# A schedule by tables: the first and last batch row scanned by column halves, and every step placed on its own

## The chip, the cores and the metric

One core of one Trainium2 chip runs the kernel. The metric is device time of one execution in microseconds: the median of three runs is 2578.41 us (2577.72 to 2578.85). Lower is better.

## The reference

The input is x of 16 batch rows by 1024 positions by 256 channels. A "row" below is one of the 16 batch rows, "columns" are its 1024 positions.

```python
x = x + 0.5 * ffn(layernorm(x))        # FFN 1
x = x + ssm(layernorm(x))              # a state-space layer
x = x + 0.5 * ffn(layernorm(x))        # FFN 2

def ffn(x):                            # hidden width 768, weights are integers / 127
    return (silu(x @ wg.T) * (x @ wu.T)) @ wd.T

def ssm(x):                            # E=256 channels, N=16 states, R=64
    z, params = x @ W_z.T, x @ W_params.T
    dt = softplus(params[..., :R] @ W_dt.T + b_dt)
    u = silu(causal_conv4(x))          # 4 taps, by channel
    A = -exp(A_log)                    # (E, N)
    a = exp(dt[..., None] * A); bt = (a - 1) / (A + 1e-10)
    # h[t] = a[t-1]*h[t-1] + bt[t-1]*u[t-1], h[0] = bt[0]*u[0], for each channel and state
    y = sum_n(C[..., n] * h[..., n])
    return ((y + u * D) * silu(z)) @ W_out.T
```

## The kernel before, in words

Channels lie on the 128 partitions in EH = 2 groups (h), columns on the free axis, in NC = 2 chunks (c) of CH = 512. For each row b and each of the 16 states s and 2 groups h there is one **unit** of the scan, 512 units in all:

- ScalarE `ex` writes exp(dt * A) of 1024 columns into one of 6 slots of `ring` (L781).
- VectorE `scan` runs TENSOR_TENSOR_SCAN over 1024 columns into PSUM (`g_bank`, L977), from `du_bank`, which ScalarE's `db` (L768) fills once for each group from GpSimd's `d`.
- VectorE `cm` multiplies by 1/A and by the C row that a DMA (`bc`) has spread over all partitions (L1008).
- GpSimd `cm` adds the product to `acc` (L856).

Around the scan of row b lie all other steps. A step is named by kind, then FFN or norm number where there is one, then row, chunk and so on. `ld` loads x (SP). `ln` (VectorE, L929 and L933), `lr` (GpSimd, L804 and L806: 1/sqrt), `ls` (VectorE, L938), `lx` (ScalarE, L624: the normed rows), `T` (TensorE transposes, L508/L511) and `Te` (ScalarE copies out) are one layer norm; `Ts` and `Tl` make a second fp16 part for the FFNs. `ga` and `up` (TensorE, L531) are the FFN's two inputs by blocks m = 0 to 5, `si` its silu, `sh` (VectorE, L948) or `sc` and `hp` (ScalarE and GpSimd, m = 0, 2, 4) the product; `dn` (TensorE, L543, 24 matmuls each) its output, `rs` and `rp` the residual. `pm`, `pe`, `cv` (L582), `us`, `dt`, `da`, `dl`, `dp`, `rm` (L597), `ai` (VectorE, L965 and L968), `u0`, `dt0`, `z`, `zs` are the state-space layer ahead of the scan; `gate` (GpSimd), `op` (TensorE, L553), `rc`, `ra` come behind it. `cw` and `bc` are the DMAs of C, `st` stores. The matmul jobs share 4 PSUM banks, each held until the step that reads it is done.

There is one order of all steps, `K.order`, made by `schedule()`: every step gets a time in units of the scan (row b begins at 32 b), the list is sorted, and each engine takes its own steps from the list in that order. Engines wait only by semaphores. So a step that waits holds back all that stands behind it on its engine, however ready that is.

Before, the times come from few numbers: a start for each kind and chunk (`AT`), a fixed pace over m (`PACE`), and lags (`LAG`). All silu steps are moved to the next slot of a grid of 4 units, `ex`, `da` and `dl` to another such grid, so that ScalarE changes its table of functions twice in 4 units (L611). All rows have the same times. SP loads x of row b into `x_in` once row b-1 is through with it, and `x_fin` holds the row that leaves.

Of the kernel before, what the change touches and what calls it, by code (L numbers as in the profile page):

```python
# [38 lines left out]
P = 128  # L39
# [37 lines left out]
AT = {  # L77
# [6 lines left out]
}  # L84

PACE = {
    "gu1": 0.732, "gu2": 1.087,
}

LAG = {  # L90
# [11 lines left out]
def phase(t, start):  # L102
    return CYCLE * ((t - start) // CYCLE) + start


def schedule():
    out = []

    def at(t, *ev):
        out.append((t, len(out), ev))  # L110

    def put(t0, name, i, *ev):
        at(t0 + AT[name][i], *ev)

    def after(t0, name, lag, i, *ev):
        at(t0 + AT[name][i] + LAG[lag][i], *ev)

    def rows(t0, f, b):
        for c in range(NC):
            put(t0, f"ln{f}", c, "ln", f, b, c)  # L120
            for kind in ("lr", "ls", "lx", "T", "Te") + (("Ts", "Tl") if f != 2 else ()):
                after(t0, f"ln{f}", f"{kind}{f}", c, kind, f, b, c)

    def curved(t, pe, act):
        p = phase(t, AT["silu"][0])
        at(p + 0.01 * (t - p), *pe)
        at(p + 0.01 * (t - p) + 0.005, *act)

    def ffn(t0, f, b):
        for c in range(NC):  # L130
            for m in range(HM):
                t = t0 + AT[f"gu{f}"][c] + m * PACE[f"gu{f}"]
                curved(t, ("ga", f, b, c, m), ("si", f, b, c, m))
                at(t + LAG["up"][0], "up", f, b, c, m)
                if m in POOLED:
                    at(t + LAG["up"][0] + LAG["sc"][0], "sc", f, b, c, m)
                    at(t + LAG["up"][0] + LAG["hp"][0], "hp", f, b, c, m)
                else:
                    at(t + LAG["up"][0] + LAG["sh"][0], "sh", f, b, c, m)
            for jp in range(2):  # L140
                put(t0, f"dn{f}", 2 * c + jp, "dn", f, b, c, jp)
                after(t0, f"dn{f}", f"rs{f}", 2 * c + jp, "rs", f, b, c, jp)
                if f == 1:
                    after(t0, f"dn{f}", "rp1", 2 * c + jp, "rp", b, c, jp)
# [893 lines left out]
```

## Time and profile before

| | |
|---|---|
| median of the runs | 2578.41 us |
| the profiled execution: its time | 2578.04 us |
| its span | 2576.0 us |
| first scan of row 0 | 135.5 us after the span's start |
| first scan of row 1 / of row 15 | 272.4 / 2374.0 us |
| `db` of row 2's second group / row 13's second group (starts) | 493.6 / 2145.8 us |
| end of the last product of the scan | 2503.3 us |

The profiled execution lies 2.0 us above its span, which is what is around the span, and 0.4 us below the median. The profile counts times from the span's start. The two cuts in the row before the last are starts of `db` 11 rows apart, so that the stretch between them is 11 whole rows.

### The profile page before, as it was taken

Reading aid. Unit: us, or ns where it says so; the run is one execution under the profiler, and the core shown is the slowest. Engines: PE = TensorE matmul, PEld = TensorE weight load, DVE = VectorE, ACT = ScalarE, POOL = GpSimd, SP = SyncE. Lnnn points to the kernel's source line nnn. Section 1 sums busy time; section 2 is a strip of 40 time slices with the busy share of each in tenths; the row PEclk is TensorE's granted clock in tenths of the full one; section 3 lists DMA queues with packets and bytes.
Section 4 is the critical chain, followed back from the end, with each engine's and each line's share of the span. In section 5 each row is a group of like instructions: output and inputs, shape, how many; then the busy total and the mean of one; then the engine's idle time right before and its main releaser. Section 6 shows DMA issues by size and latency. Waiting matters only on the chain.

```text
span 2576.0 us, 28487 instructions
## 1 busy us (share of the span) xinstructions
PE 2290.1 (89%) x9220; PEld 1382.1 (54%) x9220; DVE 2287.3 (89%) x2294; ACT 1984.9 (77%) x2830; POOL 2074.4 (81%) x1286
## 2 busy tenths in 40 slices
PE   6877799899998989999898999999899999988478
PEld 3443455556465555646555564655556565555245
DVE  2189999999999999999999999999999999999981
ACT  4668787887878788787877878787787878776643
POOL 2367988888798888879888888988888898888772
PEclk9887999999999999999999999999999999998689
DMA  2133334334343433434343343434334343433430
GB/s 73 34 118 120 131 116 130 128 118 139 108 147 116 131 130 117 139 108 147 121 132 121 119 139 107 148 121 133 122 119 139 107 147 122 133 114 115 140 115 17
DMA packets 112025, 307.97 MB, mean 120 GB/s; under 512 B 11201, under 2 KB 45314, under 8 KB 111874
## 3 DMA queue, kind: packets, MB, share of 16 engines
q1 hardware_dynamic: 111874, 306.13, 36.3%
q8 instruction: 73, 1.20, 0.2%
q14 instruction: 78, 0.64, 0.1%
HBM read 288.27 MB, written 17.83 MB: 119 GB/s over the span
## 4 chain that ended last, share of the span: by engine, by line
PE 50%; ACT 19%; DVE 13%; issue 10%; POOL 7%; DMA 1%; DVEq 0%; SPq 0%; POOLq 0%; ACTq 0%
PE work L543 19%; PE work L531 12%; DVE g_bank L977 7%; PE work L582 6%; ACT ring L781 5%; POOL acc L856 4%; PE work L511 4%; DVE ring L1008 4%; ACT normed L624 4%; PE work L553 2%; ACT L611 2%; PE work L560 2%; PE work L590 2%; ACT xt_lo L662 1%; PE work L597 1%
## 5 line engine op out<-in xcount | busy, mean ns | idle before, releaser
L856 POOL TENSOR_TENSOR acc<-acc,ring 128x1024 f32<-128x1024 f32 x512 | 1211.0, 2365 | 175.3 <-DVE ring L1008 154.8
L977 DVE TENSOR_TENSOR_SCAN g_bank<-du_bank,ring 128x1024 f32<-128x1024 f32 x512 | 1174.6, 2294 | 29.9 <-ACT du_bank L768 15.8
L543 PE MATMUL work<-wd_t,hid 128*128 128x256 f32 x3072 | 691.7, 386 | 22.2 <-DVE hid L948 18.5
L1008 DVE SCALAR_TENSOR_TENSOR ring<-g_bank,inv_a,ring 128x1024 f32<-128x1024 f32 x512 | 654.9, 1279 | 11.3
L543 PEld LDWEIGHTS work<-wd_t,hid 128*128 128x128 f32 x3072 | 596.3, 194 | 117.9 <-DVE hid L948 21.3
L781 ACT ACTIVATE ring<-dt,a_coef 128x1024 f32<-128x1024 f32 x512 | 548.0, 1138 | 1.5 <-DVE g_bank L977 0.2
L825 POOL TENSOR_TENSOR hid<-hid,sil 128x512 f32<-128x512 f32 x192 | 244.6, 1274 | 136.3 <-ACT hid L683 136.3
L531 PE MATMUL work<-xt_hi,wg_t 128*128 128x512 f16 x768 | 311.1, 405 | 42.7 <-ACT xt L649 15.7
L611 ACT ACT_TABLE_LOAD x257 | 329.7, 1283 | 4.6
L531 PE MATMUL work<-xt_lo,wg_t 128*128 128x512 f16 x768 | 310.8, 405 | 0.0
L531 PE MATMUL work<-xt_hi,wu_t 128*128 128x512 f16 x768 | 302.4, 394 | 5.3 <-ACT sil L675 5.2
L531 PE MATMUL work<-xt_lo,wu_t 128*128 128x512 f16 x768 | 302.3, 394 | 0.0
L675 ACT ACTIVATE sil<-work 128x512 f32<-128x512 f32 x384 | 220.5, 598 | 102.1 <-PE work L531 98.0
L582 PE MATMUL work<-xt,tap_diag 128*128 128x512 f32 x512 | 232.2, 596 | 0.0
L511 PE MATMUL work<-ident,normed 128*128 128x128 f32 x1024 | 139.1, 292 | 89.0 <-ACT normed L624 89.0
L948 DVE SCALAR_TENSOR_TENSOR hid<-sil,work 128x512 f32<-128x512 f32 x192 | 130.3, 678 | 93.6 <-PE work L531 93.6
L511 PEld LDWEIGHTS work<-ident,normed 128*128 128x128 f32 x1024 | 128.4, 203 | 121.8 <-ACT normed L624 108.5
L531 PEld LDWEIGHTS work<-xt_hi,wg_t 128*128 128x128 f16 x768 | 78.3, 102 | 179.5 <-issue 32.8
L582 PEld LDWEIGHTS work<-xt,tap_diag 128*128 128x128 f32 x512 | 95.5, 191 | 109.3 <-issue 97.7
L531 PEld LDWEIGHTS work<-xt_hi,wu_t 128*128 128x128 f16 x768 | 76.8, 100 | 130.3 <-issue 40.6
L691 ACT ACTIVATE x_mid<-work 128x512 f32<-128x512 f32 x64 | 37.7, 588 | 139.5 <-PE work L543 139.5
L683 ACT ACTIVATE hid<-work 128x512 f32<-128x512 f32 x192 | 112.3, 585 | 37.0 <-PE work L531 37.0
(90 smaller groups left out, 2829.2 us busy)
## 6 DMA issues: line engine op xcount, KB each, us to landing
ring<-c_rows SPq DMA_DIRECT2D x512, 512.0 KB, 3.7
x_in<-L_attn_x SPq DMA_DIRECT2D x32, 512.0 KB, 4.6
out<-x_fin SPq DMA_DIRECT2D x32, 512.0 KB, 4.0
c_rows<-params SPq DMA_DIRECT2D x32, 32.0 KB, 3.4
ring<-L_ffn_w_gate SPq DMA_DIRECT2D x1, 768.0 KB, 5.8
ring<-L_ffn_w_up SPq DMA_DIRECT2D x1, 768.0 KB, 7.2
ring<-L_ffn_w_down SPq DMA_DIRECT2D x1, 768.0 KB, 10.5
wz_t<-L_attn_W_z SPq DMA_DIRECT2D x1, 256.0 KB
```

The source lines that it names most:

```text
L511: last = pe.matmul(dst[:, j * P:(j + 1) * P], block, ident[:], start=(j == 0), stop=(j == TJ - 1))
L531: last = pe.matmul(dst[:], w[:, k, m * P:(m + 1) * P], part_[:, k, :], start=(k == 0 and i == 0), stop=(k == EH - 1 and i == 1))
L543: last = pe.matmul(dst[:, j * E:(j + 1) * E], hid[:, K.unit[f, bt, c, m] % HIDS, t:t + P], wd_t[:, m, :], start=(m == 0), stop=(m == HM - 1))
L582: last = pe.matmul(dst[:], tap_diag[:, h, k, :], xt[:, h, k + c * CH:k + (c + 1) * CH], start=(k == 0), stop=(k == KW - 1))
L611: nc.scalar.preload_act_table_set(name)
L675: nc.scalar.activation(sil[:, K.at["silu", ev][1] % SILUS, :], bank(job)[:], ACT.Silu, scale=GATE_SCALE).then_inc(freed(job), 1)
L781: nc.scalar.activation(decay[:, slot, :], dt[bt % 2][:, h, 0:L], ACT.Exp, scale=a_coef[:, h, s:s + 1]).then_inc(S["decay"], 1)
L825: nc.gpsimd.tensor_tensor(v, v, sil[:, k, :], ALU.mult).then_inc(S["product"], 1)
L856: nc.gpsimd.tensor_tensor(acc[bt % 2][:, h, :], acc[bt % 2][:, h, :], cg[:, slot, :], ALU.add).then_inc(S["summed"], 1)
L948: nc.vector.scalar_tensor_tensor(hid[:, i, :], sil[:, K.at["silu", silu][1] % SILUS, :], H_SCALE, bank(job)[:], ALU.mult, ALU.mult).then_i ...
L977: scan = nc.vector.tensor_tensor_scan(g_bank[:], du_bank[:], decay[:, a, :], 0.0, ALU.add, ALU.mult)
L1008: nc.vector.scalar_tensor_tensor(cg[:, k, :], g_bank[:], inv_a[:, h, s:s + 1], spread[:, k_c, :], ALU.mult, ALU.mult).then_inc(S["weighted ...
```

## The change

**The tables.** `AT`, `PACE`, `LAG` and both grids go. `ROW` has a position for every step of a row; `HEAD` replaces those of row 0 up to the scan, `TAIL` those of row 15 behind it. `schedule()` only adds 32 b and sorts. The number of steps is the same (5920).

**Paired rows.** In rows 0 and 15 (`paired`) a unit is no longer one group by 1024 columns: it is both groups by 512 columns. Units 0 to 15 (p = 0) do the first half of the columns, units 16 to 31 (p = 1) the second. A unit has two scans, two exps and two products of 512 columns, and one addition on GpSimd of 2 x 512. The state at column 511 is kept in `carry` by one VectorE copy in each unit of p = 0, and is the start of the scan of p = 1. With it, `d`, `db`, `gate` go by halves of the columns, and the waits of `u0`, `dt0`, `ex`, `ai`, `op` ask for one half only.

**Buffers.** Row 1's x goes into `x_fin`, so that it can be loaded at once; row 15's result goes into `x_in`.

```diff
-AT = { "scan0": [0.67, -0.01], "cm": [0.75], "bc": [-4.95], ...
-PACE = { "gu1": 0.732, "gu2": 1.087, }
-LAG = { ...
+ROW = {
+    "ln2": [-23.104, -15.157],
+    "lr2": [-23.088, -15.505],
+    "ls2": [-21.644, -14.717],
+    "lx2": [-20.845, -14.043],
+    "T2": [-18.333, -12.53],
...
+HEAD = {
+    "ln2": [-25.298, -5.26],
...
+TAIL = {
+    "op": [19.781, 20.832, 43.795, 44.13],
...
+def paired(b):
+    return b in (0, B - 1)
...
+        for name, ev in row_events(b):
+            table = HEAD if b == 0 and name in HEAD else TAIL if b == B - 1 and name in TAIL else ROW
+            i = seen[name] = seen.get(name, -1) + 1
+            out.append((round(SLOTS * b + table[name][i], 3), len(out), ev))
...
-                    if s == 0 and h == 0:
+                    if s == 0 and p == 0:
                         wait(act, "dt_first", ("dt0", bt))
+                    elif s == 0 and paired(bt):
+                        for h in range(EH):
+                            wait(act, "sp_sum", ("dp", bt, h, p))
...
+                    d = decay[:, K.number[ev[1:]] % DECAYS, :]
+                    for h in range(EH) if paired(bt) else (p,):
+                        dst, t = (halves(d)[:, h, :], slice(p * CH, (p + 1) * CH)) if paired(bt) else (d, slice(0, L))
+                        nc.scalar.activation(dst, dt[bt % 2][:, h, t], ACT.Exp,
+                                             scale=a_coef[:, h, s:s + 1]).then_inc(S["decay"], 1)
...
+                        for h in range(EH) if pair else (p,):
+                            less = EH - 1 - h if pair else 0
+                            wait(dve, "weighted", was, less=less if was and paired(was[1]) else 0)
+                            wait(dve, "decay", ("ex",) + ev[1:], less=less)
+                            g, du_h, d_h, v_h = (halves(x)[:, h, :] if pair else x for x in (g_bank[:], du_bank[:], d, v))
+                            first = [carry[:, k, s, h, :] if pair and p else 0.0 for k in range(2)]
+                            scan = nc.vector.tensor_tensor_scan(g, du_h, d_h, first[0], ALU.add, ALU.mult)
...
+                            if pair and p == 0 and h == 0:
+                                wait(dve, "scanned", ("scan",) + ev[1:])
+                                if not with_tiny:
+                                    nc.vector.tensor_copy(carry[:, 0, s, :, :],
+                                                          halves(g_bank[:])[:, :, CH - 1:CH]).then_inc(S["carried"], 1)
...
-                    wait(pe, "gated", ("gate", bt, EH - 1))
+                    wait(pe, "gated", ("gate", bt, piece(bt, EH - 1, jp // 2)))
...
+        def x_of(b):
+            return x_fin if b == 1 else x_in
+        def fin(b):
+            return x_in if b == B - 1 else x_fin
```

Sorted, the old and new positions give these orders, which the prediction refers to.

```
round the norm of FFN 1's output (row b+1 beside the scan of row b), first chunk
VectorE  old: scan9 ls3 ln2 cm9 scan10 sh ls2 cm10       new: ln2 cm9 sh scan10 cm10 ls2
GpSimd   old: cm8 hp cm9 lr2 cm10                        new: cm8 ra lr2 cm9 hp cm10
TensorE  old: up4 up5 T2 ga(FFN 2)0 ga1 dn dn pm         new: up5 ga(FFN 2)0 ga1 T2 dn dn pm
the `ai` of row b+1
VectorE  old: scan11 sh ai ai ln1 ai ai cm11             new: sh cm10 ai scan11 ai ai cm11 ai
TensorE  old: rm dt dt rm rm rm up                       new: dt rm dt rm rm up up ga rm

head, row 0, chunk 0 unless said, new
TensorE: T1, all 12 ga/up with 4 of chunk 1 among them, dn dn, up ga up up, T2, ga, pm,
         cv(h1), up, dt(h0), ga, cv(h0), up, dt(h1), rm, z, T1 of row 1, dn(c1), up ga ga of row 1, dn(c1)
ScalarE: us(h1), da dl (h0), si si (c1), us(h0), lx1 of row 1, u0, sc, Te, zs, Tl, da(h1), rs(c1), sc,
         dl(h1), si si, lx1, rs(c1), dt0, si, ex0 ex1, Te, db
         (old: both chunks and groups of da, dl and us, then dt0, ex0 to ex3, db)
tail, row 15, new
TensorE: op(c0), T3(c0) and 6 ga/up of it, row 14's last dn dn, the other 6 ga/up, op(c1), dn(c0), T3(c1), 12 ga/up, dn(c1)
         (old: row 14's last dn dn, op x4, T3(c0), FFN 2 of both chunks)
```

Between silu steps and exp or log steps, the old order has 257 changes of ScalarE's table, 16 in each middle row; the new one has 289, 18 in each.

## Rows read from the trace of the kernel before

**Rows 1.** The page: busy time of each engine, and VectorE in 40 slices

```profile
PE 2290.1 (89%) x9220; PEld 1382.1 (54%) x9220; DVE 2287.3 (89%) x2294; ACT 1984.9 (77%) x2830; POOL 2074.4 (81%) x1286
...
DVE  2189999999999999999999999999999999999981
```

**Rows 2.** Stretches: start:end, length, busy (x) per engine, PEclk, DMA share, GB/s

```profile
493.60:2145.80 1652.20, 1541.26 (x6338) 934.41 (x6337) 1569.37 (x1564) 1356.29 (x1936) 1425.83 (x881) 0.96 0.39 127
135.50:272.30 136.80, 101.56 (x316) 54.64 (x316) 132.20 (x114) 100.86 (x137) 110.00 (x64) 0.79 0.38 127
2373.40:2503.30 129.90, 73.46 (x261) 46.12 (x260) 123.16 (x94) 69.76 (x84) 97.32 (x50) 0.72 0.40 130
2503.30:2576.00 72.70, 60.95 (x284) 42.77 (x282) 11.99 (x30) 21.27 (x38) 19.77 (x16) 0.95 0.07 22
```

**Rows 3.** VectorE's waits in the 11 middle rows: total us, times, longest

```profile
DVE hid L948 <- PE work L531: 23.0, 29, 1.2
DVE shift L938 <- POOL rstd L806: 19.9, 15, 1.7
DVE acc L965 <- PE work L597: 13.9, 22, 0.9
DVE g_bank L977 <- ACT du_bank L768: 6.4, 14, 0.8
```

**Rows 4.** VectorE's groups there: busy us, mean ns, idle before

```profile
L977 DVE TENSOR_TENSOR_SCAN g_bank<-du_bank,ring 128x1024 f32<-128x1024 f32 x353 | 809.7, 2294 | 14.5 <-ACT du_bank L768 6.4
L1008 DVE SCALAR_TENSOR_TENSOR ring<-g_bank,inv_a,ring 128x1024 f32<-128x1024 f32 x352 | 450.1, 1279 | 7.5
L948 DVE SCALAR_TENSOR_TENSOR hid<-sil,work 128x512 f32<-128x512 f32 x132 | 89.5, 678 | 23.0 <-PE work L531 23.0
...
L938 DVE SCALAR_TENSOR_TENSOR shift<-meanvar,rstd 128x4 f32<-128x4 f32 x67 | 32.9, 492 | 20.0 <-POOL rstd L806 19.9
```

**Rows 5.** Timeline round one `ls` of FFN 1's output, all engines

```profile
1369.70 2.35 POOL L856 TENSOR_TENSOR acc<-acc,ring 128x1024 f32<-128x1024 f32 x1
...
1372.01 0.20 POOL L804 TENSOR_TENSOR rstd<-meanvar,eps 128x4 f32<-128x4 f32 x1
...
1373.35 0.16 DVE L938 SCALAR_TENSOR_TENSOR shift<-meanvar,rstd 128x4 f32<-128x4 f32 x1 [1.72 <-POOL rstd L806]
...
1376.21 0.98 PE L508 MATMUL work<-ident,normed 128*128 128x128 f32 x7 [3.39 <-ACT normed L624]
```

**Rows 6.** ScalarE's timeline in the head

```profile
64.88 1.06 ACT L649 ACTIVATE xt<-work 128x512 f32<-128x512 f32 x2
...
94.66 1.28 ACT L611 ACT_TABLE_LOAD   x1
95.96 0.60 ACT L744 ACTIVATE dt<-work 128x512 f32<-128x512 f32 x1
...
102.65 2.06 ACT L624 ACTIVATE normed<-x_in,shift,rstd 128x256 f32<-128x256 f32 x4
```

**Rows 7.** The chain that ended last, in the head: start, us, what

```profile
31.58 8.63 PE work L531 x40
40.21 10.36 PE work L543 x48
...
53.41 0.43 POOL x_mid L832
...
77.78 3.45 PE work L582 x8
...
135.52 2.31 DVE g_bank L977
```

**Rows 8.** The same chain in the tail

```profile
2494.85 13.45 PE work L543 x48
2508.30 5.36 PE work L553 x24
```

**Rows 9.** GpSimd's costliest group, whole run

```profile
L856 POOL TENSOR_TENSOR acc<-acc,ring 128x1024 f32<-128x1024 f32 x512 | 1211.0, 2365 | 175.3 <-DVE ring L1008 154.8 <-ACT params L735 6.5
```

More of the change, by code:

```diff
@@ L106, in schedule @@
 def schedule():
     out = []
[L109 to L144, printed above, removed]
@@ L201, in __init__ @@
         place = {ev: i for i, ev in enumerate(self.order)}
+        self.units = [(b, s, p) for b in range(B) for p in range(EH) for s in range(N)]
+        self.number = {unit: i for i, unit in enumerate(self.units)}
         uses, until = [0] * BANKS, [-1] * BANKS
@@ L398, in earlier, with halves, part, shaped @@
         def earlier(ev, back):
-            q = ev[1] * SLOTS + ev[3] * N + ev[2] - back
-            return ("cm", q // SLOTS, q % N, q % SLOTS // N)
+            i = K.number[ev[1:]] - back
+            return ("cm",) + K.units[i] if i >= 0 else None
+        def halves(t):
+            return t.rearrange("p (h t) -> p h t", h=EH)
+        def part(b, p, t, first=0):
+            if paired(b):
+                return t[:, :, first + p * CH:first + (p + 1) * CH]
+            return t[:, p, first:first + L]
+        def shaped(b, t):
+            return halves(t) if paired(b) else t
+        def x_of(b):
+            return x_fin if b == 1 else x_in
+        def fin(b):
+            return x_in if b == B - 1 else x_fin
         def bank(job):
@@ L452, in _ @@
                     wait(sp, "free", ("pm", bt, c))
-                    for i in range(SPREADS):
-                        q = EH * N - 1 - i
-                        wait(sp, f"c_spread{(bt * SLOTS + q - 2 * SLOTS) % SPREADS}", ("bc", bt - 2, q % N, q // N))
+                    for unit in [u for u in K.units if u[0] == bt - 2][-SPREADS:]:
+                        wait(sp, f"c_spread{K.number[unit] % SPREADS}", ("bc",) + unit)
                     sp.dma_start(c_rows[bt % 2, :, c * CH:(c + 1) * CH],
@@ L719, in _ @@
                     _, bt = ev
-                    wait(act, "free", ("cv", bt, EH - 1, 0))
+                    for h in range(EH):
+                        wait(act, "free", ("cv", bt, h, 0))
                     nc.scalar.activation(u[bt % 2][:, :, 1:2], u[bt % 2][:, :, 2:3], ACT.Copy).then_inc(S["u_first"], 1)
@@ L841, in _ @@
                 elif kind == "gate":
-                    _, bt, h = ev
-                    wait(pool, "summed", ("cm", bt, N - 1, h))
-                    for c in range(NC):
-                        wait(pool, "free", ("z", bt, h, c))
-                    nc.gpsimd.tensor_tensor(acc[bt % 2][:, h, :], acc[bt % 2][:, h, :], zs[:, h, :],
-                                            ALU.mult).then_inc(S["gated"], 1)
+                    _, bt, p = ev
+                    wait(pool, "summed", ("cm", bt, N - 1, p))
@@ L849, in _ @@
+                    for k in range(NC):
+                        wait(pool, "free", ("z", bt, k, p) if paired(bt) else ("z", bt, p, k))
+                    v = part(bt, p, acc[bt % 2])
+                    nc.gpsimd.tensor_tensor(v, v, part(bt, p, zs), ALU.mult).then_inc(S["gated"], 1)
                 elif kind == "cm":
-                    _, bt, s, h = ev
+                    _, bt, s, p = ev
                     wait(pool, "weighted", ev)
                     if s == 0:
-                        wait(pool, "acc_begun", ("ai", bt, h, NC - 1))
+                        for k in range(EH):
+                            wait(pool, "acc_begun", ("ai", bt, k, p) if paired(bt) else ("ai", bt, p, k))
@@ L970, in program @@
                     elif kind == "scan":
-                        _, bt, s, h = ev
-                        a = K.at["decay", ("ex",) + ev[1:]][1] % DECAYS
-                        wait(dve, "weighted", earlier(ev, 1))
-                        wait(dve, "decay", ("ex",) + ev[1:])
+                        _, bt, s, p = ev
+                        i, pair = K.number[ev[1:]], paired(bt)
+                        d, v = decay[:, i % DECAYS, :], cg[:, i % TERMS, :]
+                        was = earlier(ev, 1)
```

334 lines of the change are left out of this document (209 added, 125 removed), and 87 rows, old and new, of tables (AT, LAG, ROW, TAIL).

## The prediction

> **What bounds the kernel now.** I begin with the page: busy times and slices [rows 1]. VectorE is at 9 or more tenths in every slice from the third on; only the first slices and the last are poor. So the run has three parts: a head up to the first scan (135.5 us), sixteen rows of scan, and a tail behind the last product (2503.3 to 2576 us). The stretches give their sizes [rows 2]: 11 middle rows take 1652.2 us, 150.2 each; row 0 takes 136.8, row 15 129.9, the tail 72.7. In the middle rows VectorE works 142.7 us of 150.2 and TensorE 140.1. One is the bound and the other is right behind it, with ScalarE at 123.3 and GpSimd at 129.6. VectorE stands idle 7.5 us a row.
>
> Where these 7.5 us are is in the waits [rows 3]: 23.0 us for TensorE's `up`, 19.9 for GpSimd's 1/sqrt, 13.9 for `rm`, 6.4 for `du_bank`: 63.2 over 11 rows, 5.7 a row. The other 1.8 are small gaps between instructions, which an order doesn't touch. So 5.7 us a row is the most that a better order can win from waits, and 144.5 the shortest row. Inside the busy time there is a little more: `ls` takes 492 ns on average and the second `ai` 1274 [rows 4], but one `ls` that started late took 160 ns [rows 5]. These are stalls inside instructions, some 2 us a row for `ls` (6 x 0.33), and I expect nothing of them for the sum.
>
> **Part 1, the head.** I follow chunk 0 in the new orders. The first chunk's residual is ready at 53.84 [rows 7]. New, four instead of two jobs of chunk 1 stand ahead of `dn`: two more of four matmuls at 0.216 us (8.63 us for 40) [rows 7], 1.7 us, so 55.6. Norm, transposes and the copy to `xt` took from 53.84 to 65.94 [rows 6, 7], 12.1 us, and I keep that: 67.7. `pm` (half of a `cv`, 1.7), one `ga` (0.9) and the first `cv` (3.45 [rows 7]) end at 73.8. Before, the second chunk's `dn` of 10.36 us [rows 7] came in between; that is what the halves save first. From here ScalarE's queue counts. A plain step is 0.6 us, a table load 1.28, `lx` 2.06, one chunk of `da` and `dl` 3.35 (6.69 for two) [rows 6]. Up to `Te` of row 1: us 0.6, load 1.3, da and dl 3.35, load 1.3, two si 1.2, us 0.6, lx 2.1, u0 and sc 0.8: 85.0. It waits for TensorE's T1, behind three ga/up, two dt, cv, rm, z and T1 itself: 73.8 + 13.6 = 87.4. Then Te 1.2, zs 0.6, Tl 1.2, load 1.3, da 1.5: 93.2. `rs` needs `dn` of chunk 1: TensorE is there at 93.5. rs, sc, dl: 96.9. Load, two si, lx: 101.4; the second rs waits until 101.4 + 0.6. dt0 and si 0.8, load 1.3, four exps of half width 2.3, Te 1.2, db 1.0: the first scan is at about 109 instead of 135.5. **-26.5 us**, and with the four banks in play I give it 105 to 120. Nothing of chunk 1 vanishes: two `ai`, its norm and `ls` now lie among row 0's scans, 2 x 1.8 + 1.8 + 0.2 = **+5.5** on VectorE. TensorE's later work (some 60 us for the rest of row 0's second half up to its last `rm`) has the 65 us of the first 16 units: little slack, an upper side for the range.
>
> **Part 2, the price of a pair.** A unit was 2.294 + 1.279 us [rows 4] and becomes two scans and two products of 512 columns. A product-like instruction of 512 columns takes 678 ns [rows 4], so two cost 77 ns more than one of 1024. The trace has no scan of 512 columns: from below the same 77 ns, from above the whole 160 ns that an instruction of 4 columns takes [rows 5]. I take 120, plus 50 for two more starts: 0.25 us a unit, 8 us a row. The 16 copies into `carry` are tiny: 0.16 each, 2.6. **+10.6 us** in row 0 and in row 15 each; bounds 5 and 16. Less than none is excluded, as nothing is removed.
>
> The Trainium skill (VectorE: DVE Perf Modes, "The TRN2 errata") puts an instruction's fixed part at about 150 cycles, 0.16 us; by it the pair would cost 12.5 us a row and the sum would be 4 us longer. The product's rows show half of that.
>
> ScalarE's exps also double in number, and it has 26.9 us free in a row; `bc` moves the same bytes in one row of halves; GpSimd's additions keep their 2.37 us [rows 9].
>
> **Part 3, the fourteen rows between.** Here the order alone changes. I look at the largest single wait. VectorE's `ls` stood 1.72 us for GpSimd, whose 1/sqrt began at 1372.01, behind an addition to `acc` that started at 1369.70 [rows 5]; between `ln2` and `ls2` VectorE's own order has a product, a scan and an `sh`. And TensorE then stood 3.39 us before `T2` for the same chain. New, `lr2` stands ahead of that addition, `ls2` behind a whole product more, and `T2` behind an `up` and two `ga`. That wait goes, 1.8 us a row with its smaller kin, and TensorE wins 3 us with it, which comes back to VectorE as earlier `up`s. Of the wait for `up` (2.1 a row) I take 1.1 as gone. `rm`: new, the four `ai` are spread, but the last `rm` stands behind two `up` and a `ga`; 1.3 a row, of which I take 0.3. `du_bank`: 0.6, I take 0.3. Together 3.5 of 5.7 us a row. The cover for all this is TensorE, which would be busy 140.1 of 146.7. Two more table loads a row, 2.6 us, lie on ScalarE and are hidden by its 26.9 free microseconds. **-49 us** for 14 rows; ends: 0 and -80.
>
> The `x_fin` and `x_in` edits cost nothing, since the loads are off the path; without that cover they would cost one load's landing.
>
> **Part 4, the tail.** Before, 72.7 us: row 14's last `dn` on TensorE until 2508.3, four `op` 5.36, a norm, two chunks of FFN 2 [rows 2, 8]. New, row 15's first half is through `gate`, `op` and norm by then. Behind the last product TensorE has: `dn` of row 14, 5.0; 6 ga/up 5.2; two `op` 2.7; `dn` of chunk 0 10.4 [rows 7]; T3 and its second part about 4; 12 ga/up 10.4; `dn` 10.4; then `rs` and the store 4.7. That is 53. The second half's own chain (addition, gate, op, norm) takes about 20 us and is done when TensorE reaches T3. **-19.7 us**; bounds 47 and 62 for the tail. The first half's norm moves into row 15's scans, +2.0.
>
> **The sum.** Row 1 begins at 109 + 136.8 + 10.6 + 5.5 = 261.9 instead of 272.3: -10.4. Rows 1 to 14: -49. Row 15: +12.6. Tail: -19.7. Together -66.5 from the span of 2576.0: 2509.5, and 2.0 around it: 2511.5. The profiled run lies 0.4 us under the median of the runs, so I say **2512 us**.
>
> **The rivals.**
> A: the middle rows win nothing. For it: TensorE is only 2.6 us a row behind VectorE, and at its clock between two levels (PEclk 0.96) it may be the true bound; each wait that goes comes back as one of VectorE for TensorE. Against: TensorE stands idle 10.1 us a row, much of it in the chain of `ls`. Then 2512 + 49 = 2561.
> B: all 63 us of waits per 11 rows go: 14 x 5.7 = 80, and 2481.
> C: the head gains nothing, since a ScalarE step with chunk 1's work ahead of it (both `rs` stand ahead of `dt0`) holds the first scan at 135: 2512 + 26 = 2538.
> D, slower: ScalarE's two more table loads fall where TensorE waits for a bank, so that 2.6 us a row come onto VectorE's path and no wait goes. It decides from 1.8 us a row upward: without part 3 the change is -17.5, so 14 rows must lose 22 to come out 0.2% slower. With 2.6: 2561 + 36 = 2597. Against it: between load and next step there is 0.02 us [rows 6], and ScalarE's free time is ten times the addition.
> The Trainium skill (ScalarE: Activation LUTs, "What ACT_TABLE_LOAD costs") adds 1.38 us of drain to each load; by it D's price would be 5.3 us a row. This trace disagrees: the step behind the load starts at once.
>
> **Chances.** Forecast 0.45, A 0.18, B 0.2, C 0.1, D 0.07. The range takes B with a good head at its low side and A with a dear pair at the high: 2460 to 2570; D lies outside. About 0.2% (5 us) is what a measurement can tell from no change. Faster 0.91, same 0.03, slower 0.06.
>
> **What would show it.** In the new profile: the first scan at 105 to 120 us; half scans of 1.2 us and copies of 0.1 to 0.2; starts of row 1 and row 15's `db` 14 x 146.7 us apart; `ls` without a wait of 1.7 us; 289 table loads; a tail of 53 us. I am wrong if the row stays at 150 (A), if VectorE's waits for `up` grow as those for 1/sqrt go, or if row 0 is longer than 153 us because TensorE is late with its second half.

## The result, and the profile after

The changed kernel takes 2454.95 us (median of 4 runs, 2452.45 to 2457.36) against 2578.06 beside it (2575.96 to 2578.85). The ratio is 0.9524, interval 0.9507 to 0.9540. I had said 2512 with a range from 2460 to 2570: the sign is right, but the gain is 123 us and not 66, and the time lies 5 us below the range.

The page after, whose rows answer to [rows 1], and with them the clock:

```profile
PE 2258.3 (92%) x9220; PEld 1359.8 (55%) x9220; DVE 2282.8 (93%) x2454; ACT 2030.5 (83%) x2926; POOL 2073.5 (84%) x1286
...
DVE  2599999999999999999999999999999999999993
...
PEclk9997999999999899999999899999999999999789
```

VectorE's busy time is the same as before (2287.3), so the 120 us of span that went were all time in which it stood. Four stretches show where. First row 0 up to the first scan of row 1, then fourteen rows, row 15, and the tail; the columns are those of [rows 2]:

```profile
102.14:248.31 146.17, 114.30 (x358) 57.00 (x356) 141.37 (x198) 123.73 (x195) 117.42 (x71) 0.85 0.23 68
248.31:2277.76 2029.45, 1941.13 (x7999) 1172.60 (x7998) 1978.43 (x1968) 1746.99 (x2476) 1809.05 (x1115) 0.97 0.39 130
2277.76:2406.20 128.44, 82.99 (x332) 53.90 (x332) 128.00 (x181) 85.23 (x130) 102.55 (x56) 0.83 0.23 70
2406.20:2455.60 49.40, 43.31 (x206) 30.35 (x204) 9.26 (x20) 12.66 (x23) 13.54 (x10) 0.98 0.10 33
```

The same stretch of fourteen rows before:

```profile
272.39:2373.96 2101.57, 1954.92 (x7993) 1182.51 (x7994) 1993.35 (x1968) 1716.43 (x2445) 1811.41 (x1116) 0.96 0.39 126
```

| part | before, us | after | change | forecast |
|---|---|---|---|---|
| up to the first scan | 135.5 | 102.1 | -33.4 | -26.5 |
| row 0 | 136.9 | 146.2 | +9.3 | +16.1 |
| rows 1 to 14 | 2101.6 | 2029.5 | -72.1 | -49 |
| row 15 | 129.3 | 128.4 | -0.9 | +12.6 |
| tail | 72.7 | 49.4 | -23.3 | -19.7 |
| span | 2576.0 | 2455.6 | -120.4 | -66.5 |

The miss is in rows 0 and 15 (20 us) and in the middle rows (23 us); 10 us are head and tail. VectorE's waits in 11 middle rows after, against [rows 3]:

```profile
DVE hid L1099 <- PE work L662: 11.6, 16, 1.5
DVE acc L1118 <- PE work L728: 6.7, 6, 2.6
DVE x_fin L1107 <- PE work L674: 3.4, 4, 1.4
```

That is 21.7 us where 63.2 stood. The list of TensorE leads to another step; its waits in those 11 rows, before:

```profile
PE work L508 <- ACT normed L624: 50.2, 22, 3.4
PE work L511 <- ACT normed L624: 21.3, 22, 1.0
PE work L531 <- ACT xt L649: 11.8, 11, 1.7
PE work L573 <- ACT xt L649: 8.6, 11, 0.8
PE work L597 <- ACT sp_r L747: 7.6, 22, 0.4
```

and after:

```profile
PE work L674 <- DVE hid L1099: 21.5, 9, 3.3
PE work L662 <- ACT xt_lo L793: 8.0, 11, 0.7
PE work L662 <- ACT sil L806: 7.6, 11, 0.7
PE work L662 <- ACT hid L814: 7.6, 11, 0.7
PE work L639 <- ACT normed L755: 6.9, 11, 0.6
```

Before, TensorE stood 71.5 us ahead of its transposes for ScalarE's `lx` (`normed`); after, 6.9. The sum of its waits is 110.6 before (two more, 5.9 and 5.2) and 65.4 after (four more: 5.0, 4.6, 4.0, 0.2). The row stretch is 52.3 us shorter (1652.2 against 1599.9, from `db` to `db`), the waits are 45 us less, and TensorE's busy time is 8.8 less, at a granted clock of 0.97 of full speed instead of 0.96. These two make up the 52.3 us to within 2. That says where the time was, and not yet why it went: an engine's waits and work always add up to its stretch. VectorE's account closes as well (41.5 us of waits and 9.4 of work less). Which list leads to the cause, the runs below have to show.

One pair (a unit of two column halves) after, on VectorE's timeline:

```profile
102.14 2.35 DVE L1142 TENSOR_TENSOR_SCAN g_bank<-du_bank,ring 128x512 f32<-128x512 f32 x2 [0.53 <-ACT du_bank L903]
104.40 0.73 DVE L1178 SCALAR_TENSOR_TENSOR ring<-g_bank,inv_a,ring 128x512 f32<-128x512 f32 x1
105.04 0.15 DVE L1183 COPY carry<-g_bank 128x2 f32<-128x2 f32 x1
105.11 0.74 DVE L1178 SCALAR_TENSOR_TENSOR ring<-g_bank,inv_a,ring 128x512 f32<-128x512 f32 x1
105.76 1.22 DVE L1142 TENSOR_TENSOR_SCAN g_bank<-du_bank,ring 128x512 f32<-128x512 f32 x1
```

A pair with its copy goes from 102.14 to 105.76: 3.62 us. A bare unit of 1024 columns takes 3.65 from start to start. Each of the five instructions begins before the one ahead of it is recorded as ended.

### The profile page after: what moved, and what is told of

Same layout as the page of the kernel before. It is cut to its first block and busy times, and to the rows that moved or that the text cites. A ratio compares the mean times of both kernels' runs of the same rounds, so it can differ in the third digit from the quotient of the medians.

```text
span 2455.6 us, 28769 instructions
## 1 busy us (share of the span) xinstructions
PE 2258.3 (92%) x9220; PEld 1359.8 (55%) x9220; DVE 2282.8 (93%) x2454; ACT 2030.5 (83%) x2926; POOL 2073.5 (84%) x1286
## 5 line engine op out<-in xcount | busy, mean ns | idle before, releaser
L1142 DVE TENSOR_TENSOR_SCAN g_bank<-du_bank,ring 128x1024 f32<-128x1024 f32 (+1 forms) x512 | 1100.6, 2155 | 7.3 <-ACT du_bank L903 0.5
L1178 DVE SCALAR_TENSOR_TENSOR ring<-g_bank,inv_a,ring 128x1024 f32<-128x1024 f32 (+1 forms) x576 | 664.6, 1159 | 11.4
L674 PEld LDWEIGHTS work<-wd_t,hid 128*128 128x128 f32 x3072 | 590.0, 193 | 153.4 <-DVE hid L1099 43.6
L921 ACT ACTIVATE ring<-dt,a_coef 128x1024 f32<-128x1024 f32 (+1 forms) x576 | 577.4, 1047 | 7.0 <-DVE g_bank L1142 4.1
L662 PE MATMUL work<-xt_hi,wg_t 128*128 128x512 f16 x768 | 299.7, 390 | 29.4 <-ACT sil L806 14.5
L662 PE MATMUL work<-xt_lo,wg_t 128*128 128x512 f16 x768 | 298.8, 389 | 0.0
L964 POOL TENSOR_TENSOR hid<-hid,sil 128x512 f32<-128x512 f32 x192 | 249.7, 1301 | 53.6 <-ACT hid L814 38.9
L684 PE MATMUL work<-wo_t,acc 128*128 128x256 f32 x512 | 119.0, 386 | 11.3 <-POOL acc L987 6.1
```

Source lines behind the costliest of these rows:

```text
L662: last = pe.matmul(dst[:], w[:, k, m * P:(m + 1) * P], part_[:, k, :], start=(k == 0 and i == 0), stop=(k == EH - 1 and i == 1))
L674: last = pe.matmul(dst[:, j * E:(j + 1) * E], hid[:, K.unit[f, bt, c, m] % HIDS, t:t + P], wd_t[:, m, :], start=(m == 0), stop=(m == HM - 1))
L921: nc.scalar.activation(dst, dt[bt % 2][:, h, t], ACT.Exp, scale=a_coef[:, h, s:s + 1]).then_inc(S["decay"], 1)
L964: nc.gpsimd.tensor_tensor(v, v, sil[:, k, :], ALU.mult).then_inc(S["product"], 1)
L1142: scan = nc.vector.tensor_tensor_scan(g, du_h, d_h, first[0], ALU.add, ALU.mult)
L1178: nc.vector.scalar_tensor_tensor(v, g, inv_a[:, h, s:s + 1], c_row, ALU.mult, ALU.mult).then_inc(S["weighted"], 1)
```

## The experiments

**The pair alone.** The old order and its three tables, with the new loops for rows 0 and 15:

```diff
-ROW, HEAD, TAIL and their schedule()
+AT, PACE, LAG and their schedule()
 def paired(b): return b in (0, B - 1)
```

> Rows 0 and 15 by column halves and the new buffers, but every step at its old position. The old positions put the whole of row 0 ahead of its first scan and row 15's op behind its last gate, so nothing can start earlier; what is left is the price of 64 paired units. Theory F (a pair is free, because the fixed part of an instruction hides behind an independent one before it; in the new trace a paired unit comes every 3.62 to 3.66 us, one of 1024 columns every 3.65): 2578 us, give or take 3. The prediction's price (0.25 us a unit and 0.16 a copy, 10.6 a row): 2599 us. Theory F says that half of the miss in rows 0 and 15 is this term.

2582.14 us (2580.74 to 2582.97, 10 runs), ratio 1.0017, interval 1.0008 to 1.0027. Row 0 of it, from its first scan to that of row 1, and row 15, from its first scan to the last product:

```profile
138.14:275.97 137.83, 99.64 (x317) 55.03 (x318) 134.55 (x194) 106.47 (x166) 109.89 (x65) 0.80 0.22 71
2377.77:2508.14 130.37, 71.72 (x267) 46.11 (x266) 125.98 (x173) 74.79 (x111) 96.75 (x50) 0.76 0.22 69
```

Row 0 is 1.0 us longer than the 136.9 of before and row 15 1.1 longer than 129.3, where I had put 10.6 each. Of the 4.6 us in the span 2.6 are the first scan, which begins at 138.1. Pairs alone gain nothing, and cost about 1 us a row.

**The order alone.** `ROW` for all sixteen rows, no pairs:

```diff
-    return b in (0, B - 1)
+    return False
-            table = HEAD if b == 0 and name in HEAD else TAIL if ... else ROW
+            table = ROW
```

> Only the table ROW, for all 16 rows, no pairs. If the middle rows' 5.15 us a row come from the order inside a row and from nothing at the ends, 14 rows give -72, and rows 0 and 15 some more: 2495 to 2510 us. Rival (the middle gains because the early head lets TensorE run ahead): the rows stay near 150 and the time near 2560.

2494.39 us (2493.89 to 2498.31), ratio 0.9684, interval 0.9668 to 0.9700. Rows 1 to 14 take 144.7 us each from `db` to `db`, against 145.0 in the changed kernel, so the middle's gain is all here. The tail is 73.8 us, near the 72.7 of before.

**Without the head's table, and without the tail's.**

```diff
-HEAD if b == 0 and name in HEAD else TAIL if ... else ROW
+TAIL if b == B - 1 and name in TAIL else ROW      # the first
+HEAD if b == 0 and name in HEAD else ROW          # the second
```

> The changed kernel, but row 0 has the positions of ROW up to its scan, too; pairs and TAIL stay. If HEAD is what brings the first scan from 135.5 to 102.1 us, this loses most of 33 us less what row 0 then saves in work moved: 2478 to 2490 us, first scan at about 130. Rival (pairs alone, by their narrower waits, start the scan early): 2455 to 2462.

> The changed kernel, but row 15 has the positions of ROW behind its scan too; pairs and HEAD stay. If TAIL is what shortens the tail from 72.7 to 49.4 us: 2476 to 2480 us, a tail of some 72 us. Rival (the narrower waits of op alone shorten it): under 2465.

Without `HEAD` 2473.50 us (2470.26 to 2479.44), ratio 0.9601, interval 0.9584 to 0.9618. The first `db` starts at 130.3 instead of 101.1, but its row 0 is 137.6 us long from `db` to `db`, against 145.3: `HEAD` brings the scan forward by 29 us and gives 18.5 in the end. 7.7 us go back into row 0, which takes over chunk 1's work. Another 5.0 are in rows 1 to 14, which are that much shorter without `HEAD` (2025.0 us against 2030.0), and no run says why. Without `TAIL` 2476.77 us (2474.43 to 2478.82), ratio 0.9608, interval 0.9592 to 0.9624; the tail is 69.0 us. So the two tables for the edges carry 40 us. In the old order the pairs gave nothing without them; the two tables without pairs were not run.

**One step moved before.** My text put 1.8 us a row on `ls2` waiting for `lr2`, so I moved `lr2` alone:

```diff
-    "lr2": [0.22, 0.11],
+    "lr2": [0.05, 0.11],
```

> The kernel before with one lag changed: GpSimd's lr2 of the first chunk stands ahead of the addition to acc, not behind it (0.22 becomes 0.05). This takes away the 1.72 us wait of ls in each row and nothing else. Theory V (VectorE is the bound, a wait of it is worth its length): 16 x 1.7 = 27 us, so 2551. Rival T (TensorE is right behind, the wait comes back as waits for up or rm): under 10 us, 2568 to 2578.

2577.41 us (2573.94 to 2578.95, 10 runs), ratio 0.9998, interval 0.9988 to 1.0007. VectorE's wait for 1/sqrt falls from 19.9 to 2.7 us in 11 rows, and nothing is won. Its timeline at the place of [rows 5]:

```profile
1369.75 2.35 POOL L856 TENSOR_TENSOR acc<-acc,ring 128x1024 f32<-128x1024 f32 x1
...
1370.33 1.78 DVE L938 SCALAR_TENSOR_TENSOR shift<-meanvar,rstd 128x4 f32<-128x4 f32 x1
...
1370.52 1.28 ACT L611 ACT_TABLE_LOAD   x1
...
1371.82 1.15 ACT L781 ACTIVATE ring<-dt,a_coef 128x1024 f32<-128x1024 f32 x1
...
1372.88 2.06 ACT L624 ACTIVATE normed<-x_mid,shift,rstd 128x256 f32<-128x256 f32 x4
...
1374.98 1.09 PE L508 MATMUL work<-ident,normed 128*128 128x128 f32 x8 [3.39 <-ACT normed L624]
```

Two things are to be seen. `ls` (here the 4-column product at L938) starts 0.58 us after a GpSimd addition and ends with it: the wait has become a stall inside the instruction (its mean rises from 492 to 749 ns). And it didn't matter: ScalarE has a table load and an `ex` ahead of `lx`, and works through them without a pause, so that `lx` comes 0.77 us after `ls` has ended. TensorE stands 3.39 us before `T2`, as in [rows 5]. TensorE's whole list of waits is as before (50.2 and 21.3 for `normed`).

**The same step moved back in the changed kernel.**

```diff
-    "lr2": [-23.088, -15.505],
+    "lr2": [-22.65, -15.505],
```

> The changed kernel with lr2 of the first chunk put back behind that addition. The new VectorE order has a product, an sh, a scan and a product between ln2 and ls2, 5.5 us, and product, addition and 1/sqrt take 1.3 + 2.4 + 1.3 = 5.0, so by the rows no wait should come back: 2455 to 2460. Rival (the place of lr2 is what won the 1.8 us a row): 2455 + 26 = 2481.

2458.94 us (2453.16 to 2461.18), ratio 0.9532, interval 0.9516 to 0.9548: it costs nothing that can be told.

**Pairs in all rows, and pairs in series.**

```diff
 def paired(b):
-    return b in (0, B - 1)
+    return True
```

and, on top of it, each half's product right behind its own scan:

```diff
-scan h=0, scan h=1, product h=0, product h=1
+scan h=0, product h=0, scan h=1, product h=1
```

> The changed kernel with every row scanned by column halves, 512 paired units instead of 64. Theory F (a pair is free on VectorE): 2450 to 2465, if ScalarE's 512 more exps (about 2 us a row) stay hidden. The prediction's price of 10.6 us a row: 14 x 10.6 = 148 more, 2603.

> As all_rows_paired, but VectorE's four instructions of a unit stand as scan, product, scan, product, each product right behind the scan that it reads; the same instructions and numbers. Theory F says the pair is free because neighbours that don't depend on each other overlap by some 0.09 us while a dependent one starts 0.03 late: two dependent neighbours more in a unit, 2 x 0.12 x 512 = 120 us slower than all_rows_paired. Rival (half instructions are simply cheap, in whatever order): the same time as all_rows_paired, within 10 us.

2530.82 us (2530.36 to 2531.22), ratio 0.9818, interval 0.9802 to 0.9835; in series 2697.26 us (2692.45 to 2699.37), ratio 1.0466, interval 1.0449 to 1.0484. With pairs everywhere a row is 149.8 us, and VectorE is busy in 98% of it:

```profile
468.30:2123.60 1655.30, 1545.38 (x6337) 919.84 (x6336) 1623.30 (x2443) 1441.50 (x2310) 1423.97 (x881) 0.97 0.23 71
```

So a pair costs 1 us a row at the edges, and 5 in the middle, between my two expectations. Counting the neighbours explains most of it. In the kernel before, 26 of row 0's 32 products come directly behind their scan, and 25 scans directly behind a product; each of them starts 0.035 us late, and in pairs it starts some 0.085 early. In the changed kernel's 11 middle rows it is 253 of 352 products and 132 scans, so 35 places a row instead of 51: other instructions stand between, and a pair has less to hide. And `ls` is back at 473 ns from 175, 1.8 us a row. In series a bare unit takes 4.04 us, and the kernel 166 us more than with interleaved halves, where I had expected 120:

```profile
1245.36 1.23 DVE L1142 TENSOR_TENSOR_SCAN g_bank<-du_bank,ring 128x512 f32<-128x512 f32 x1
1246.62 0.75 DVE L1178 SCALAR_TENSOR_TENSOR ring<-g_bank,inv_a,ring 128x512 f32<-128x512 f32 x1
1247.29 1.22 DVE L1185 TENSOR_TENSOR_SCAN g_bank<-du_bank,ring 128x512 f32<-128x512 f32 x1
1248.55 0.75 DVE L1178 SCALAR_TENSOR_TENSOR ring<-g_bank,inv_a,ring 128x512 f32<-128x512 f32 x1
1249.21 0.15 DVE L1191 COPY carry<-g_bank 128x2 f32<-128x2 f32 x1
1249.40 1.23 DVE L1142 TENSOR_TENSOR_SCAN g_bank<-du_bank,ring 128x512 f32<-128x512 f32 x1
```

A product that needs the scan just ahead of it starts 0.03 us after the scan's end (1246.59 to 1246.62). A scan that needs nothing of the product ahead starts 0.08 us before the product's end. The order of the four decides what halves cost: these two runs have the same instructions, two to a scan and two to a product.

**`ls` rewritten.** To take its stall away, four instructions with one input column and a scalar replace it:

```diff
-nc.vector.scalar_tensor_tensor(shift[:, slot, :], meanvar[:, slot, :, 0], -1.0, rstd[:, slot, :], ...)
+for j in range(TJ):
+    nc.vector.tensor_scalar(shift[:, slot, j:j + 1], meanvar[:, slot, j, 0:1], -1.0,
+                            rstd[:, slot, j:j + 1], ALU.mult, ALU.mult)
```

> The kernel before with ls written as four tensor_scalar instructions, the one factor as a scalar per partition, so that none reads two tensors. In the trace of before an ls that meets a GpSimd instruction ends when that ends (1431.71 + 1.03 = 1432.74, GpSimd's ended at 1432.72). Theory L (the two engines lock each other out, and the lock costs VectorE its time): ls falls from 492 ns to some 0.25 us for all four, 2 us a row less: 2578 - 25 = 2553. Rival (as with lr2, the time is spent elsewhere): 2578.

> Both edits of ls in the kernel before: lr2 ahead of the addition, and ls as four instructions. Moving lr2 alone turned 17 us of waits into 16 us of longer ls instructions. Theory L: with the lock gone too, wait and stall are both won, 19.9 + 22 us in 11 rows, some 55 in 16: 2525 to 2535. Rival T (TensorE is the bound right behind): no faster than before_ls_alone by more than 5 us.

2581.17 us (2579.34 to 2582.94, 10 runs), ratio 1.0013, interval 1.0004 to 1.0023; with `lr2` moved too 2578.59 us (2576.59 to 2578.88), ratio 1.0002, interval 0.9992 to 1.0011. The four take 37 us in 11 rows where the one took 32.9, so VectorE was not relieved, and these runs don't decide by themselves. In all four kernels with the old order the 11 rows stay at 1651.4 to 1652.2 us, while VectorE's work in them goes from 1569 to 1584.

**No lock in the changed kernel.** `ls` as above, and the first product behind `rm` left in its PSUM bank, so that the second reads only one operand from SBUF:

```diff
-first ai:  t <- bank * u        second ai: t <- u * D - t
+first ai:  bank <- bank * u     second ai: t <- u * D - bank
```

> The changed kernel with ls as four instructions and with the first product of ai left in its PSUM bank, so that the second reads one tensor of SBUF and one of PSUM; same results. There the second ai takes 1665 ns instead of the 750 of one that meets no GpSimd instruction: 64 x 0.9 = 58 us of VectorE's time. Theory L with VectorE as the bound: 2455 - 45 = 2410. Theory T (TensorE, busy 96% in the middle rows, takes over): 2435 to 2450.

2460.12 us (2459.07 to 2464.66), ratio 0.9541, interval 0.9525 to 0.9557. The second `ai` falls from 1727 to 748 ns, and the wait for `rm` rises to 30.9 us in 11 rows. VectorE works 19.6 us less in them (the four instructions of `ls` take part of the relief back), and they are 3.2 us shorter; the first scan is 6 us later. Nothing is won, which neither theory had.

**Fewer matmuls.** The last of six hidden blocks is left out of both down projections, so a sixth of the hidden width is missing from the output:

```diff
 for m in range(HM):
+    if m == HM - 1: continue
     last = pe.matmul(dst, hid[:, unit[m], t:t + P], wd_t[:, m, :], ...)
```

> The changed kernel without the last of the six blocks that each dn sums (the output lacks a sixth of the hidden width): 7 us a row less for TensorE, nothing less for the others. If VectorE is the bound of the middle rows, only its waits for TensorE go, 21.7 us in 11 rows, and half the ends' matmuls: 2420 to 2435. If TensorE is the bound: 16 x 7 = 112 less, under 2380.

2452.54 us (2450.23 to 2455.58), ratio 0.9510, interval 0.9494 to 0.9526: within what can be told from the changed kernel, and outside both of my ranges. Two groups of TensorE in 11 rows, here and in the changed kernel:

```profile
L676 PE MATMUL work<-wd_t,hid 128*128 128x256 f32 x1760 | 395.0, 382 | 18.1 <-DVE x_fin L1109 10.7 <-DVE hid L1101 7.4
...
L715 PE MATMUL work<-xt,tap_diag 128*128 128x512 f32 x353 | 162.3, 607 | 27.1 <-ACT sil L808 27.1
```

```profile
L674 PE MATMUL work<-wd_t,hid 128*128 128x256 f32 x2112 | 475.3, 384 | 21.5 <-DVE hid L1099 21.5
...
L713 PE MATMUL work<-xt,tap_diag 128*128 128x512 f32 x354 | 158.8, 595 | 4.6 <-ACT sil L806 4.6
```

80 us of `dn` went. TensorE's busy time falls by half of that only, from 1532.4 to 1493.7, since other matmuls got dearer at a granted clock of 0.95 instead of 0.97. And its idle time rises by 41 us, with 27.1 us for ScalarE's silu ahead of `cv` as the largest wait.

**A two-by-two of the orders.** Either the units' own steps (`bc`, `ex`, `db`, `d`, `scan`, `cm`, `gate`) or all the others go back to their old places, in all rows and without pairs; in the third run only what TensorE and ScalarE do outside the units goes back:

```diff
-            table = ROW
+            table = OLD if name in OLD else ROW
```

> All rows by the new row table and no pairs, but the units' own steps (bc, ex, db, d, scan, cm, gate) stand where the old tables had them, against all the others (both row transforms, feed-forwards, projections, convolution), which stand at their new places. The same rows with all steps at new places took 2494 us, with all at old places 2577. Theory U (the gain of the middle rows is in how the units are spaced within the row, closer at its end than in its middle): it is lost here, 2555 to 2580. Rival O (it is in the places of the other steps): it stays, 2490 to 2510. Rival J (neither alone, the two fit together): slower than 2580.

> The other half: the units' own steps at their new places, all other steps at their old ones, no pairs. Theory U: 2490 to 2515. Rival O: 2555 to 2580. Rival J: slower than 2580, and with the run beside it the two halves don't add up to 83 us.

> All rows by the new row table and no pairs, with TensorE's and ScalarE's steps outside the units at their old places, while VectorE's, GpSimd's and the units' own stand at the new ones. If what is won is the order on VectorE and GpSimd, this takes 2490 to 2520; if it is the order on TensorE or ScalarE, 2550 or more.

| units' steps | the others | us | ratio, interval |
|---|---|---|---|
| old | old | 2578.26 | (before) |
| new | new | 2494.39 | 0.9684 (0.9668 to 0.9700) |
| old | new | 2916.45 | 1.1315 (1.1296 to 1.1334) |
| new | old | 2820.75 | 1.0940 (1.0922 to 1.0958) |
| new | TensorE's and ScalarE's old | 2876.54 | 1.1156 (1.1137 to 1.1175) |

Rival J holds: the gain has no half to which it belongs. Steps are 1 to 4 units apart from where they were, and all three mixtures make waits by the hundred microseconds: with the units' steps old, VectorE waits 124.1 us for `up` and 112.5 for `dn` in 11 rows.

**A shorter product on VectorE.** The second `ai` on 8 of 512 columns; 504 columns of the D-skip and the sign are left out:

```diff
+t = t[:, 0:8]
-nc.vector.scalar_tensor_tensor(t, u[..., 2 + c * CH:2 + (c + 1) * CH], d_skip, t, ...)
+nc.vector.scalar_tensor_tensor(t, u[..., 2 + c * CH:10 + c * CH], d_skip, t, ...)
```

> The changed kernel with the second of the two products behind rm cut from 512 to 8 columns, so that 504 columns of the D-skip and the sign are left out: it took 1727 ns, four times a row, 108 us in 64 of them. It takes some 1.5 us of VectorE's work off each, 6 us a row, and with it the stretches in which that product and GpSimd stop each other, while every wait for rm stays as it was. If VectorE's own work is what the rows take, some 85 to 95 us go: 2360 to 2375. If the rows are held by a chain through several engines in which rm and what follows it are a link, about half or less goes, 2400 to 2440. If it is neither, within 2450 to 2460, as with fewer matmuls.

2426.29 us (2424.71 to 2428.19), ratio 0.9412, interval 0.9397 to 0.9428. Its product still takes 828 ns on 8 columns, so 0.9 us went and not 1.5: 39.6 us in 11 rows, of which the stretch gained 21.3 (1578.6 against 1599.9). TensorE's waits there say which 21:

```profile
PE work L662 <- ACT xt_lo L793: 8.0, 11, 0.7
...
PE work L674 <- DVE hid L1099: 0.2, 1, 0.2
```

TensorE's wait before `dn` for VectorE's `sh` falls from 21.5 to 0.2 us; the others and TensorE's busy time (1532.2) stay. The gain is that wait to a tenth of a microsecond. VectorE's own wait for `rm` meanwhile rises from 6.7 to 29.3, so that half of its relief comes back as waiting. The total is in the range that I gave to a chain through several engines.

**Both reliefs, and a shorter softplus.** The product on 8 columns together with the left-out hidden block; and, in the changed kernel, ScalarE's Exp and Ln and GpSimd's first step of each softplus on 8 of 512 columns, so that dt is not the softplus:

```diff
-activation(y, y, ACT.Exp, scale=-1.0);        activation(sp_l, sp_l, ACT.Ln);        tensor_tensor(sp_l, sp_l, sp_v, ...)
+activation(y[:, 0:8], y[:, 0:8], ACT.Exp, scale=-1.0); ... the same for the other two
```

> Both reliefs at once on the changed kernel: the second product behind rm on 8 of 512 columns, and the sixth hidden block left out of both down projections. Alone they gave 29 us and 3 us. Theory B (the rows are bounded by VectorE and TensorE together, each ready to take over when the other gets less): together they give far more than the sum of 32, 2360 to 2395. Theory C (a chain that goes round all engines by the order of the steps): about the sum, 2418 to 2428.

> The changed kernel with the third and the last of ScalarE's steps of a softplus (Exp, Ln) and the first of GpSimd's three on 8 of 512 columns, so that dt is not the softplus: some 1.0 us of ScalarE's work and 1.1 of GpSimd's less, four times a row, and the first decay of a row's channel group comes earlier. Theory B: VectorE and TensorE keep all their work, within 2440 to 2458. Theory C: this chain is a link of it (GpSimd waits for ScalarE's Ln 36 us in 11 rows), so some 20 us or more go, below 2438.

Both together 2434.54 us (2426.00 to 2436.50), ratio 0.9436, interval 0.9414 to 0.9457: theory B is wrong. The matmuls left out add nothing to the shorter product's 2426.29; three of the four executions are 8 us or more above it, so theory C's range (2418 to 2428) is missed too. The shorter softplus takes 2466.59 us (2465.77 to 2469.04), ratio 0.9571, interval 0.9555 to 0.9587: less work on two engines, and 12 us slower than the changed kernel's 2454.95, which neither theory had. Its `ls` and second `ai` on VectorE in 11 rows:

```profile
L1121 DVE SCALAR_TENSOR_TENSOR acc<-u,d_skip,acc 128x512 f32<-128x512 f32 x44 | 58.9, 1340 | 1.6
L1089 DVE SCALAR_TENSOR_TENSOR shift<-meanvar,rstd 128x4 f32<-128x4 f32 x67 | 32.5, 484 | 0.0
```

`ls` is back from 175 ns to 484: one of the six in a row takes 1.93 us again (at 637.94, for one), which eats the 17 us that the second `ai` gained. TensorE stands 15.2 us for ScalarE's `u`, which wasn't in its list. This tells why nothing was won in these 11 rows, which are 3.6 us longer. The rest of the loss is outside them: rows 1, 13 and 14 are 9.8 us longer together, and I have no cause for it.

## Why the prediction missed

The forecast for the span was 54 us too high: 20 of them are the first step below, 23 the second, and 10 lie in head and tail.

**The pair's price** (part 2) is the first step that failed, by some 20 us. I put 0.25 us on a pair and 0.16 on a copy. Measured: 3.62 us for a pair with its copy, against 3.65 for the bare unit; 1.0 and 1.1 us for the two rows with pairs alone. The terms themselves were near: a half product takes 734 ns, a half scan 1212 (1272 with a carried state), the copy 149. Durations add up to 4.04 us, though. What I missed is that neighbours that don't depend on each other overlap in the record by about 0.09 us each, while in the unit of before the product waits for its scan, and the next scan for the product. Row 0 then is 9.3 us longer, some 8 of them for the moved work (I had 5.5 for that), and in row 15 the moved work took VectorE's idle time: it works 128.0 of 128.4 us where it worked 123.2 of 129.9.

**The middle rows** (part 3) are the second, and here the mechanism as I told it is wrong, though the size came within a third. I took the largest single wait, VectorE's for `lr2`, as cause, and TensorE's 3.39 us before `T2` as its consequence. Moving `lr2` took the first away and left the second untouched. The cause of the second stood in the same timeline: ScalarE's queue had a table load and an `ex` between the transposes' copies and `lx2`, and the old order had too few matmuls ahead of `T2` to last that long. That this also accounts for the gain is read from the orders and the lists, and no run moves these steps alone. In the new order the first `T2` stands 2.6 units later in the row and its `lx2` 0.5, both `T1` about 2 units later, so that other matmuls fill the time: 71.5 us for `normed` in 11 rows become 6.9. What I had read, that TensorE is 2.6 us a row behind VectorE, made me call VectorE the bound. The run with the shorter product shows how the two hang together: VectorE lost 40 us of work and the stretch 21.3, as much as TensorE's wait for `sh` was long. The chain of waits through the middle rows of before would have pointed to TensorE; it is the view that I read only at head and tail. Its first line, from 493.6 to 2145.8:

```profile
by line: PE work L543 20.5%; PE work L531 14.1%; issue 8.1%; PE work L582 6.9%; ACT ring L781 6.0%; DVE g_bank L977 5.0%; PE work L511 4.5%; ACT normed L624 3.7%; PE work L553 2.9%; POOL acc L856 2.9%; DVE ring L1008 2.7%; ACT L611 2.3%; PE
```

TensorE has 48.9% in the lines shown, VectorE 7.7. My upper bound of 5.7 us a row was a sum of VectorE's waits and so no bound of the right thing: in the 11 rows VectorE's work fell too, by 9.4 us. That the 14 rows gained 5.1 each, and so less than the bound, is no support for it.

**The head** (part 1) was 7 us too late, and all of it is there by the end of the first norm. After, the residual is ready at 51.4 and `xt` at 60.3, where I had 55.6 and 67.7: 4.2 us ahead of the norm and 3.2 in it. I had added 1.7 us ahead of `dn`, which in fact begins at 38.8 and not at 40.1; and what I kept of the old order held two waits behind a `hid` product on GpSimd (`hp`). In the kernel before, it stands ahead of the residual, and another one ahead of `lr2`, which waits 2 us for it:

```profile
52.15 1.27 POOL L825 TENSOR_TENSOR hid<-hid,sil 128x512 f32<-128x512 f32 x1 [4.77 <-ACT hid L683]
53.37 1.27 POOL L832 TENSOR_TENSOR x_mid<-x_mid,x_in 128x512 f32<-128x512 f32 x1
```

Its end, 54.64, is when the residual was ready; the 53.84 that I took from [rows 7] is only where the chain leaves it. After (the first line GpSimd's, the second ScalarE's):

```profile
50.10 1.27 POOL L971 TENSOR_TENSOR x_mid<-x_mid,x_in 128x512 f32<-128x512 f32 x1 [3.92 <-ACT x_mid L822]
...
59.21 1.06 ACT L780 ACTIVATE xt<-work 128x512 f32<-128x512 f32 x2
```

From there my walk keeps its distance to the end (first scan 102.1, forecast 109). **The tail** came to 49.4 us where I had 53: row 14's last `dn` is through 0.8 us behind the last product and not 5.0. The other way, two `op` take 3.5 us and not 2.7: the 5.36 us of [rows 8] are 24 matmuls, and so three `op` and not four.

**Smaller slips**, none of which moves the forecast by more than a microsecond. VectorE is at 9 or more tenths from the fourth slice on and not from the third; the three terms of +5.5 add up to 5.6; D decides from 22 / 14 = 1.6 us a row and not from 1.8. The second `ai` (L968) is not among [rows 4]; its line is below. And `bc` moves half the bytes in rows 0 and 15 (DMA share 0.23 instead of 0.38 in row 0), since both groups read one C row.

**The rivals.** A, C and D did not come. B had the right size for the middle rows (5.7 a row, with 5.1 measured) by the wrong account. D's table loads, 289 now, cost nothing that the list of waits shows, and the stall of `ls`, of which I expected nothing, is gone (492 to 175 ns), but the second `ai` took it over (1274 to 1727 ns, before and after); the two cancel (-21 and +20 us in 11 rows).

```profile
L968 DVE SCALAR_TENSOR_TENSOR acc<-u,d_skip,acc 128x512 f32<-128x512 f32 x44 | 56.1, 1274 | 1.6
```

```profile
L1121 DVE SCALAR_TENSOR_TENSOR acc<-u,d_skip,acc 128x512 f32<-128x512 f32 x44 | 76.0, 1727 | 1.6
```

**What stays open.** Rows are not bound by one engine. Less work on VectorE gave half of itself back, less on TensorE nothing, less on ScalarE and GpSimd cost time. I can say which wait each run lost or gained, but not derive from the order alone how long a row will be, nor why the row without the sixth block waits for ScalarE's silu. Which of the moved steps are needed to take the transposes' waits away I did not isolate: all three mixtures cost more than the order gains, and TensorE's steps alone at new places were not tried.

## What to carry to other kernels

Where two engines are within a few per cent of each other, read the waits of both, and follow the chain of waits through the stretch that is to shrink, before pricing a wait. A wait that a second queue covers is worth nothing: look at what else stands ahead of the step that uses the result. Splitting an instruction in two costs little if the halves are interleaved so that no instruction needs its neighbour's result, and if the whole ones did need it; in series the same halves cost 166 us more here. This order, fitted as a whole, could not be taken over by halves.

## What the hardware showed beyond that

**Neighbours overlap on VectorE.** In these traces independent instructions start about 0.09 us before the recorded end of the one ahead, a dependent one 0.03 us behind it. The Trainium skill (VectorE: DVE Perf Modes, "The TRN2 errata") has a fixed part of about 150 cycles, 0.16 us, for each instruction. In durations the runs come near it (two half products take 1468 ns, 189 more than the 1279 of the whole), but on the path the price of 12.5 us a row that I worked out from it did not appear: a row of pairs cost 1.0 and 1.1 us.

**VectorE and GpSimd stop each other.** A product of 4 columns (`ls`) took between 0.15 and 1.94 us. In the kernel before, 38 of them took over 0.4 us, and each of these ends within 0.06 us of the end of a GpSimd instruction. One of them:

```profile
1431.62 1.10 POOL L815 TENSOR_TENSOR dt<-sp_l,dt 128x512 f32<-128x512 f32 x1
1431.71 1.03 DVE L938 SCALAR_TENSOR_TENSOR shift<-meanvar,rstd 128x4 f32<-128x4 f32 x1
```

The two end at 1432.72 and 1432.74. The form of `ai` with one operand in PSUM took 748 ns on average instead of 1727. That is what the Trainium skill (SBUF — State Buffer, "SBUF: two separate sides") says of a port pair that a VectorE instruction with two SBUF inputs and a GpSimd instruction lock against each other; the traces agree. The stall stands in the profile as busy time, not as a wait.

**TensorE's clock takes part of a relief back.** With a sixth of `dn` left out, the matmuls of `cv`, unchanged, took 607 ns instead of 595, at a granted clock of 0.95 instead of 0.97, which is a mean over stretches at its two levels of 1.2 and 2.4 GHz; in the mixtures, where TensorE stood most, it was 0.89 to 0.93 over the same rows.

**Table loads on ScalarE.** Each takes 1.28 us, before and after, and the next step starts 0.01 us behind it where it waits for nothing else.
